# Sequence-major rows in the tiles of a decoder's first attention layer, and the division by the input scales on GpSimd

## The reference, cut to what matters

```python
x = x + _L0_attn_ref(_layernorm(x), weight_qkv, weight_proj)
#   seq, batch, hidden = x.shape: attention runs over the FIRST axis (16 long, causal),
#   one independent batch entry for each of the 112 positions; 16 heads of 32, 4 key-value heads
x = x + _L0_xattn_ref(_layernorm(x), ctx, ...)
#   ln_out = _ln(x, ln_w, ln_b)
#   for each of q, k, v and qx:  y = bf16(clip(ln_out / in_scale, -448, 448)); xq = fp8_roundtrip(y)
```

## Time and profile before

| | us |
|---|---|
| median of 3 runs (4169.55, 4177.32, 4178.12) | 4177.32 |
| profiled execution, its own time | 4168.15 |
| its span in the trace | 4166.4 |
| opening block | 0 to 27 |
| loop of the first layer, first scores to the last product with values | 39 to 397 |
| rest of the first layer | 397 to 461 |
| x and the first weights loaded, first work of the self phase | 509 |

### The profile page before, as it was taken

One profiled execution on the slowest core, in us unless ns is written; L12 is line 12 of the kernel. 1 busy time (PEld: TensorE's weight loads), 2 busy tenths in 40 slices (PEclk: granted clock), 3 DMA queues, 4 the chain that ended last, 5 costly groups with the idle time before them and its releaser, 6 DMA issues. The chain is left out here.

```text
span 4166.4 us, 56017 instructions
## 1 busy us (share of the span) xinstructions
PE 3584.3 (86%) x18548; PEld 2878.3 (69%) x18548; DVE 2548.7 (61%) x6497; ACT 1715.6 (41%) x3862; POOL 771.4 (19%) x881
## 2 busy tenths in 40 slices
PE   6887089779869999969999996999959979997999
PEld 5676077567647777747777774888847766665887
DVE  3788578578756666656666666799745552225532
ACT  3666244344333434333443433588423433332222
POOL 0101044334412222212222221200312210000000
PEclk8776599889989999989999998999979989999999
DMA  4000300100020000010000003899720004332100
GB/s 155 11 9 13 114 0 0 36 25 0 0 87 25 18 25 24 17 70 26 24 18 24 25 8 113 300 404 398 265 93 1 1 1 127 112 112 98 40 9 18
DMA packets 84838, 296.76 MB, mean 71 GB/s; under 512 B 9104, under 2 KB 15248, under 8 KB 79328
## 3 DMA queue, kind: packets, MB, share of 16 engines
q1 hardware_dynamic: 78288, 276.45, 18.6%
q0 software_dynamic: 6400, 18.36, 1.4%
HBM read 252.57 MB, written 42.21 MB: 71 GB/s over the span
## 5 line engine op out<-in xcount | busy, mean ns | idle before, releaser
L39 PE MATMUL bank<-cross_w,cross_ctx_part 128*125 128x512 f32 x2304 | 593.5, 409 | 11.4 <-DVE cross_qn L883 6.8
L39 PEld LDWEIGHTS bank<-cross_w,cross_ctx_part 128*125 128x125 f32 x2304 | 426.0, 187 | 132.9 <-DVE cross_qn L883 9.0
L39 PE MATMUL bank<-self_w,self_xq 128*112 128x512 f32 x1024 | 268.4, 411 | 102.6 <-ACT self_xq L780 102.6
L889 DVE TENSOR_REDUCE cross_neg_max<-bank 112x1 f32<-112x375 f32 x256 | 133.2, 530 | 294.6 <-PE bank L699 291.9
L39 PEld LDWEIGHTS bank<-self_w,self_xq 128*112 128x112 f32 x1024 | 177.7, 181 | 154.2 <-ACT self_xq L780 103.5
L815 ACT ACTIVATE cross_prob<-bank,cross_neg_max 112x375 f32<-112x375 f32 x256 | 147.4, 576 | 323.1 <-DVE cross_neg_max L889 323.1
L39 PE MATMUL bank<-moe_wt,moe_zT 128*128 128x448 f32 x1176 | 265.8, 375 | 2.1 <-DVE moe_zT L1460 1.5
L1455 DVE TENSOR_TENSOR moe_wt<-moe_raw,moe_wt 128x1792 fp32r<-128x1792 f32 (+1 forms) x111 | 233.1, 2107 | 21.3 <-ACT moe_wt L1362 20.3
L39 PEld LDWEIGHTS bank<-moe_wt,moe_zT 128*128 128x128 f32 x1176 | 216.1, 190 | 18.2 <-issue 1.7
L39 PE MATMUL bank<-mlp_zT,mlp_signs 128*128 128x448 f32 x1024 | 221.4, 369 | 4.7 <-DVE mlp_zT L2069 4.7
L1362 ACT ACTIVATE moe_wt<-moe_raw 128x1792 fp32r<-128x1792 f32 (+1 forms) x111 | 196.9, 1776 | 48.0 <-DMA moe_raw<-in_moe_w 39.8
(11 more groups left out here) (391 smaller groups left out, 7895.7 us busy)
## 6 DMA issues: line engine op xcount, KB each, us to landing
moe_raw<-in_moe_w SPq DMA_DIRECT2D x74, 896.0 KB, 8.0
moe_raw<-in_moe_w SPq DMA_DIRECT2D x37, 1024.0 KB, 9.1
stream<-in_L1f SPq DMA_DIRECT2D x32, 768.0 KB, 4.4
cross_ctx_raw<-in_ctxT SPq DMA_DIRECT2D x32, 750.0 KB, 4.2
wide_ctxT<-in_ctxT SPq DMA_DIRECT2D x16, 750.0 KB, 12.6
wide_ctx_rows<-in_ctx SPq DMA_DIRECT2D x16, 750.0 KB
expert_rows<-a_zeros SPq DMA_DIRECT2D x1, 8960.0 KB, 26.6
moe_zrow<-expert_rows SPq DMA_DIRECT2D x35, 256.0 KB, 8.0
```

The source lines that it names most:

```text
L39: mm = pe.matmul(out, a, b, start=first and n == 0, stop=last and n == len(pairs) - 1)
L889: dve.tensor_reduce(neg_max[:, HS * t:HS * (t + 1)], score_bank(t)[0:S, 0:HS * NK].rearrange("p (h n) -> p h n", h=HS), AX.X, ALU.max, neg ...
```

## The change

The rows of a tile are ordered sequence by sequence: row = sequence * 8 + position. The host lays the input out so, the mask becomes "same position, not a later sequence" (a fill and one affine select for each of the 16 diagonals), `x1` becomes [sequence, position, feature], and `round_back` writes runs of 8 positions. The division by the scales moves: ACT applies ln_w and ln_b once while it takes z2T out of PSUM (four activations), and POOL makes all 16 pieces of y with one product of z2T and the inverse scales, both read as broadcasts. The scalings on ACT are gone.

```diff
@@ open_first_layer, gpsimd
-            pool.memset(mask[:], 0.0).then_inc(s["made"], 1)
+            pool.memset(mask[:], MASKED).then_inc(s["made"], 1)
...
-            pool.affine_select(out=mask[:], in_=mask[:], compare_op=ALU.is_ge, fill=MASKED, base=0,
-                               pattern=[[-1, P]], channel_multiplier=1).then_inc(s["masked"], 1)
-            pool.wait_ge(s["masked"], 2)
-            pool.affine_select(out=mask[:], in_=mask[:], compare_op=ALU.is_ge, fill=MASKED, base=15,
-                               pattern=[[B, P // B], [0, B]], channel_multiplier=-1).then_inc(s["masked"], 1)
+            for b in range(B):
+                pool.affine_select(out=mask[:], in_=mask[:], compare_op=ALU.not_equal, fill=0.0, base=-8 * b,
+                                   pattern=[[-1, P]], channel_multiplier=1).then_inc(s["masked"], 1)
+                pool.wait_ge(s["masked"], b + 2)
@@ open_first_layer, vector
-            dve.wait_ge(s["masked"], 3)
+            dve.wait_ge(s["masked"], B + 1)
...
-            dve.reciprocal(inverse[:], cols[:, IN_SCALE:IN_SCALE + 16]).then_inc(s["products"], 1)
+            dve.reciprocal(in_inverse[:], cols[:, IN_SCALE:IN_SCALE + 16]).then_inc(s["products"], 1)
...
-            for out, at in ((in_scale, LN_W), (in_bias, LN_B)):
-                dve.tensor_tensor(...)
+            dve.tensor_copy(ln_cols[:], cols[:, LN_W:LN_W + 2 * DC]).then_inc(s["products"], 1)
@@ first_layer, sync
-                sp.dma_start(x1[t * P:(t + 1) * P, :], xt[:, t, :]).then_inc(s["x_stored"], 16)
+                sp.dma_start(x1[:, 8 * t:8 * t + 8, :], xt[:, t, :]).then_inc(s["x_stored"], 16)
@@ first_layer, gpsimd
+            def scale_rows(t):
+                pool.wait_ge(s["z2T_taken"], t + 1)
+                wait(pool, s["shifted"], t - 1)
+                pool.tensor_tensor(y[:, t % 2].rearrange("p v (c t) -> p v c t", c=DC),
+                                   z2T[:, None, :, :].to_broadcast([P, 4, DC, T]),
+                                   in_inverse[:].rearrange("p (v c) -> p v c", c=DC)[:, :, :, None]
+                                   .to_broadcast([P, 4, DC, T]), ALU.mult).then_inc(s["scaled"], 1)
             for t in range(NT):
                 for n, ready, done in ((0, "vareps1", "rooted1"), (1, "vareps2", "rooted2")):
...
+                if t:
+                    scale_rows(t - 1)
+            scale_rows(NT - 1)
@@ first_layer, scalar
             def take_z2T(t):
                 act.wait_ge(s["z2T_in_psum"], t + 1)
-                wait(act, s["scaled"], 4 * t)
-                act.activation(z2T[:], tiled(6), ACT.Copy).then_inc(s["z2T_taken"], 1)
-            def scale_rows(t, kinds):
...
+                wait(act, s["scaled"], t)
+                for c in range(DC):
+                    op = act.activation(z2T[:, c, :], tiled(6)[:, c, :], ACT.Identity, scale=ln_cols[:, c:c + 1],
+                                        bias=ln_cols[:, DC + c:DC + c + 1])
+                op.then_inc(s["z2T_taken"], 1)
...
-                if t >= 3:
-                    scale_rows(t - 3, (2, 3))
...
-                if t >= 2:
-                    scale_rows(t - 2, (0, 1))
             out_high(NT - 1)
-            scale_rows(NT - 3, (2, 3))
             for t in range(NT - 2, NT):
                 take_z2T(t)
-                scale_rows(t, range(4))
@@ first_layer, vector
             def shift(t):
-                dve.wait_ge(s["scaled"], 4 * t + 4)
+                dve.wait_ge(s["scaled"], t + 1)
...
-                    dve.tensor_tensor(out[:, :, :, 8 * t:8 * t + 8].rearrange("p b c s -> p c s b"),
-                                      shifted[:, v].rearrange("p (c s b) -> p c s b", s=8, b=B),
-                                      magic[:, v].rearrange("p (c s b) -> p c s b", s=8, b=B),
+                    dve.tensor_tensor(out[:, :, :, 8 * t:8 * t + 8].rearrange("p b c s -> p c b s"),
+                                      shifted[:, v].rearrange("p (c b s) -> p c b s", b=B, s=8),
+                                      magic[:, v].rearrange("p (c b s) -> p c b s", b=B, s=8),
                                       ALU.subtract).then_inc(s["rounded"], 1)
@@ cross_attention_layer
-                            loads=[(x, x1.rearrange("(s b) d -> s b d", b=B))] if opening else ())
+                            loads=[(x, x1.rearrange("b s d -> s b d"))] if opening else ())
@@ decoder and host
-        x1 = nc.dram_tensor("x_after_L0_attention", (S * B, D), F32, kind="Internal").ap()
+        x1 = nc.dram_tensor("x_after_L0_attention", (B, S, D), F32, kind="Internal").ap()
-    lay["x_by_position"] = a["x"].transpose(1, 0, 2).reshape(1792, 512)
+    lay["x_by_position"] = a["x"].reshape(16, 14, 8, 512).transpose(1, 0, 2, 3).reshape(1792, 512)
```

More of the change, by code:

```diff
@@ L988, in cross_attention_layer @@
 def cross_attention_layer(k, x, io, x1, phase, xq, products_of):
-    raw_scale, in_scale, in_bias, smooth_inverse, proj_scale, head_ln = products_of
+    raw_scale, in_inverse, ln_cols, smooth_inverse, proj_scale, head_ln = products_of
     if True:
@@ L2157, in open_first_layer @@
         ve = k.sb(ctx, "open_ve", [P, NT], F32)
-        inverse = k.sb(ctx, "open_inverse", [P, 16], F32)
         block = ctx.enter_context(nc.Block())
@@ L2220, in _ @@
             dve.tensor_copy(head_ln[:], cols[:, HEAD_LN:HEAD_LN + 8]).then_inc(s["products"], 1)
-            dve.wait_ge(s["products"], 5)
-            for out, at in ((in_scale, LN_W), (in_bias, LN_B)):
[L2223 to L2226, removed]
+            dve.tensor_copy(ln_cols[:], cols[:, LN_W:LN_W + 2 * DC]).then_inc(s["products"], 1)
+            dve.wait_ge(s["products"], 6)
             for n in (0, 4):
@@ L2229, in _, with first_layer @@
                     .then_inc(s["squared"], 1)
-            dve.wait_ge(s["squared"], 4)
+            dve.wait_ge(s["squared"], 2)
             dve.wait_ge(s["weight_low"], len(pieces))
     k.recycle_semaphores()
-def first_layer(k, xt, x1, xq, xq_dram, wqkv, wo, mask4, ident16, in_scale, in_bias, zeros):
+def first_layer(k, xt, x1, xq, xq_dram, wqkv, wo, mask4, ident16, in_inverse, ln_cols, zeros):
     nc, ps = k.nc, k.ps
@@ L2636, in decoder @@
             products_of = [k.sb(cross, n, shape, F32) for n, shape in (
-                ("raw_scale", [P, 4, DC]), ("in_scale", [P, 16]), ("in_bias", [P, 16]), ("smooth_inverse", [P, 32]),
+                ("raw_scale", [P, 4, DC]), ("in_inverse", [P, 16]), ("ln_cols", [P, 8]), ("smooth_inverse", [P, 32]),
                 ("proj_scale", [P, 1]), ("head_ln", [P, 8]))]
```

## The result

The changed kernel takes 4120.32 us (median of four runs, 4103.33 to 4122.71), the kernel before beside it 4173.43: ratio 0.9852, 95% interval 0.9835 to 0.9869, about 62 us faster by that ratio. The two medians themselves lie 53 us apart, a quotient of 0.9873 that lies just outside the interval, so the ratio on record is not simply that of the medians. The runs spread over 9 us before and 19 us after; the gain is best taken as 53 to 62 us. The profiled execution is the quickest of the four, 4103.33, span 4101.6.

A forecast was written before the change was run, and what follows sets the result against it. A chain across engines, with eight ACT scalings (3.18 us) ahead of the exponentials, was taken to set the loop's period. 39.4 + 3.1 + 17.4 + 5 - 3.0 = 62 off the median 4177.3 gave 4115, range 4088 to 4150.

The forecast's parts named there:

- The loop: Nine tiles, mask 3 to mask 12: three at 20.85 us, six at 24.2, gain 39.4; ends 29 and 60.
- That POOL must not be late: Loop condition: POOL's product takes 4.35 us and ends at 224.5, so `shift` starts at 226.0 as before.
- The last two tiles: Tiles 12 and 13: 3.18 us for tile 12, 0 taken for tile 13; gain 3.1.
- After the loop: Last product with values to last `round_back`: earlier `scale_out`, faster writes, less POOL's product; gain 17.4 us, range 11 to 21.
- the -4.35: After the loop, tile 12: its product starts only after tile 13's root, just ahead of its `shift`; loss 4.35 us.
- The -2.2 of tile 11: After the loop: half of tile 12's loss of 4.35 us taken for tile 11 as well.
- The load of x: Before the next stage: runs of 2 KB instead of 32 KB load faster; gain 5 us, bounds -1 and 6.
- The opening: Start of the layer: sixteen chained selects 0.43 us apart delay DVE's statistics to 10.6; loss 3.0 us, at least 1.5.
- Clock: Rival, chance 0.14: in the loop all nine tiles get the fast product with the values; 4095 us.
- POOL late: Rival, chance 0.08: POOL's product costs 8.7 us, `shift` starts 4.35 later, no fast tiles; 4161 us.
- the slow writes: Rival, chance 0.06: `round_back` stays at 2.24 us and DVE sets 24.3 a tile; 4150 us.
- the bound on POOL: Rival, chance 0.04: POOL's product becomes the bound and the kernel slower; at 13 us a product, 4221 us.

The follow-up runs named there:

- after_again: The changed kernel once more, unchanged, for a second profile: 4106.83 us.
- x_split: The changed kernel with the load of x as sixteen DMAs, one per sequence, in place of one: 4129.42 us, one run.
- deferred_and_cast: The changed kernel with x awaited by DVE before its first addition and the mask's cast behind the first statistics: 4107.62 us, ratio 0.9816 to the kernel before.
- order_alone: The kernel before with the new row order alone, the scalings staying on ACT: 4163.1 us, ratio 0.9954.
- pool_alone: The changed kernel with the old row order, so only the product on GpSimd is new: 4154.01 us, ratio 0.9931 to the kernel before.
- before_again: The kernel before once more, unchanged, for a second profile: 4180.99 us.

## Why the prediction was right, point by point

The sum was 62 us; the ratio gives 62, the two medians 53, the two profiled executions 65. The forecast time, 4115, is 5 us from the median measured. So the mechanism was right, but that sum and ratio agree to the microsecond is luck: terms of the sum were off both ways and cancelled.

*The loop, 39.4 from three short and six long tiles.* Both forms came as foreseen (20.9 for 20.85, 24.0 for 24.2); `after_again` has tiles of 19.1 and 20.0 besides. How many of the nine would be short was a guess. It is no property of the kernel: the seven profiles of this first layer have four, four, two, two and three times none. Four give a gain of 43.7, none gives 31.6, where the sum had 29 for that case. The 31.6 come without any change in the mix; the rest is the clock's. The same holds for mask 0 to mask 3, where 6.4 us came in the profiled execution that the prediction did not have, with the same two forms of product, and none in x_split. The rest of the kernel was 11 us slower than in the first profile of the kernel before and 3 us quicker than in the second.

*That POOL must not be late.* 4.35 us was taken for the product; it is 3.61, and `shift` starts without a wait. DVE is held as foreseen. The slack was worked out as 2.3 us against `scale_out`; it is 1.8, against `add_out`, which the budget left out.

*`round_back`* was taken as 0.74 and is 0.60 to 0.69. The budget that followed (DVE waits for PE) is what the profile shows.

*The last two tiles, 3.1.* 5.7 in the profiled execution, 3.2 in x_split and `deferred_and_cast`, 5.7 to 6.3 in the other four profiles of this first layer.

*After the loop, 17.4.* Measured 21.4: too small by 4. `order_alone` gives 22.2 for the writes and the wait of `scale_out` (the sum had 5.1 + 17.9 = 23.0), so the product on GpSimd costs only 0.8 there, where the sum had -0.9 + 4.35 + 2.2 = 5.65. DVE's rows say which of the three was wrong. With the scalings on ACT and the new order, DVE waits for them 1.93, 0.18 and 8.13 us ahead of the last three `shift`:
```profile
410.94 0.69 DVE L2567 TENSOR_SCALAR a_y<-a_y 128x2048 bf16<-128x2048 bf16 x1 [1.93 <-ACT a_y L2464]
...
421.33 0.69 DVE L2567 TENSOR_SCALAR a_y<-a_y 128x2048 bf16<-128x2048 bf16 x1 [0.18 <-ACT a_y L2464]
...
436.93 0.69 DVE L2567 TENSOR_SCALAR a_y<-a_y 128x2048 bf16<-128x2048 bf16 x1 [8.13 <-ACT a_y L2464]
```
With the product on POOL it waits 0, 4.23 and 6.43. Tile 12 costs 4.05, as the -4.35 had it. Tile 13 gains 1.7, not 0.9, as the product is shorter than was taken. The -2.2 of tile 11 was the wrong one: its wait of 1.93 went, against some 1.5 for which `normalise_again` is held beside POOL. These three come to 1.9; DVE's wait for `out_high` of the last tile is 1.0 shorter (1.83 for 2.88), which leaves about the 0.8 measured. In the old order (`pool_alone`) this stretch is 4.2 longer than before.

*The load of x, 5. This step failed.* "3.67 MB at the one is 14.9 us, at the other 9.6": the rate of writes in 2 KB rows was carried over to a load, and the length of the runs was held to be what kept the load at 246 GB/s. It lands 19.9 us after its issue in the old layout and 20.1 in the new one, up to 22.7 in other executions. What holds it is its 112 partitions: 15.2 us with 128, in one execution.

*The opening, -3.0, at least 1.5.* The selects run 0.36 apart, not 0.43, and DVE's statistics start at 9.37, not 10.6, so 1.7 us late. Up to mask 0 the profiled execution loses only 0.5, `x_split` 1.8 and `order_alone` 2.0; between the two profiles of the kernel before this piece differs by 0.8 as well.

*The rivals.* "Clock" came true for four tiles of nine at most, and for none in three of the seven profiles. POOL late, the slow writes and the bound on POOL are excluded by 3.61, 0.60 and the rows of DVE. The base from the median, 4177.3, was the right one: the profiled 4168.15 lay 9 under it, and its expert stage was 13.6 us shorter than in `before_again`.

## What to carry to other kernels

Where two limits lie close together, price each part of a change alone and then both: here the new row order alone moved nothing in the loop and still gave what was gained behind it. A term that hangs on the granted clock should be given as a range between the executions that show its ends, since one profile shows only one of them. When an engine takes on more work, ask of every step behind it in its order who waits for that step, in the last tiles too: `add_out` was left out twice here. And before a load is relaid, compare its rate with one that differs in a single thing: the wait for it was worth more (11 us by waiting later) than its layout.

## What was not expected of the hardware

The same 3584 KB in 2 KB pieces: about 390 GB/s into 128 partitions, about 240 into 112, with the DMA engines busy throughout in both. Runs of 32 KB in place of 2 KB gave little: 19.7 to 19.9 us against 20.1 to 22.7.

A write of bf16 that steps to another place with every element took 2.24 us per 512 elements; with eight neighbours in a row it took 0.60 from start to start, and the dense sum of `shift` takes 2.29 for 2048, 0.57 per 512.

A product of 2048 elements with two broadcast operands takes 3.61 us on GpSimd, 1.76 ns per element, under the 2.12 of a subtraction with 896; on DVE 2.28.

One program on one core does not repeat to better than about 0.5%, in both kernels (4166.9 to 4185.7 us and 4103.3 to 4122.7). Where the granted clock falls against the tiles differs from one execution to the next, and the same nine tiles take 203.6 us at a mean granted clock of 0.84 and 216.0 at 0.78.
